# First batch of a state-space and expert layer: step size of batch two moved from POOL to VectorE, its silu in two places, four weight splits moved up

## The reference

```python
def attn(x):                                    # 8 heads of 64, state of 64
    z = x @ Wz                                  # 128 -> 256
    ssm_in = x @ Win                            # B (64), C (64), dt_raw (8), X (512)
    delta = softplus(dt_raw + dt_bias)          # the step size, per token and head
    y = ssd_scan(X, delta, B, C, A_log) + D_param * X
    z_gated = silu(z) @ Wzg                     # 256 -> 512
    return (y * z_gated) @ Wout                 # 512 -> 128
x1 = layernorm(x + attn(x))
# 12 experts, each 128 -> 512 -> 128; three routers take the top 3 and softmax them
h = gelu(sum_e dw1[:, e] * (x1 @ W1[e].T))
y = sum_e dw2[:, e] * (h @ W2[e].T) + dw3 @ b2
out = layernorm(x1 + y)
```

## Time and profile before

| what | value |
|---|---|
| median of 3 runs | 1566.34 us |
| lowest and highest | 1566.17, 1568.41 us |
| the profiled execution's own time | 1565.38 us |
| its span, first to last instruction | 1563.7 us |
| mean granted TensorE clock | 0.998 of full speed |
| busy: TensorE, VectorE, POOL, ScalarE | 1545.0, 1108.0, 663.7, 598.1 us |

### The profile page before, as it was taken

How to read it: one execution, slowest core, us unless ns; L and a number is a source line. 1 busy time by engine, 2 the same in 40 slices (tenths; PEclk the granted TensorE clock), 3 DMA queues, 4 the chain that set the end, 5 groups by cost and what they waited for, 6 DMA issues and landing times.

```text
span 1563.7 us, 25298 instructions
## 1 busy us (share of the span) xinstructions
PE 1545.0 (99%) x8634; PEld 1249.2 (80%) x8634; DVE 1108.0 (71%) x3108; ACT 598.1 (38%) x1362; POOL 663.7 (42%) x755
## 2 busy tenths in 40 slices
PE   8999999999999999999999999999999999999998
PEld 6778788888888878888788888878888788887876
DVE  7577676877768687676776768777686776867755
ACT  6652424425144351533425244242443515335130
POOL 7681623616145270643616336162451715436040
PEclk9999999999999999999999999999999999999999
DMA  5350312304023040321403123040230403214020
GB/s 176 102 158 22 116 41 66 98 29 132 19 76 88 29 135 14 103 69 46 118 17 118 44 66 98 29 128 22 71 93 29 136 14 99 73 40 125 15 74 7
DMA packets 81600, 114.79 MB, mean 73 GB/s; under 512 B 10160, under 2 KB 37312, under 8 KB 81472
## 3 DMA queue, kind: packets, MB, share of 16 engines
q1 hardware_dynamic: 81472, 113.18, 24.9%
HBM read 108.02 MB, written 5.13 MB: 72 GB/s over the span
## 4 chain that ended last, share of the span: by engine, by line
PE 92%; POOL 4%; issue 1%; DVE 1%; DMA 1%; ACT 0%; SPq 0%; POOLq 0%; DVEq 0%; ACTq 0%
PE exp_bank L246 22%; PE exp_bank L248 22%; PE exp_bank L247 22%; PE mix_bank L893 4%; PE mix_bank L919 3%; PE mix_bank L246 3%; PE mix_bank L247 3%; PE mix_bank L248 3%; PE mix_bank L901 3%; PE mix_bank L790 1%; PE turn_bank L1224 1%; POOL w_lo L445 1%; PE mix_bank L738 1%; POOL Wt L853 1%; PE mix_bank L1010 1%
## 5 line engine op out<-in xcount | busy, mean ns | idle before, releaser
L1167 POOL TENSOR_TENSOR sp_lo<-fbuf,sp_hi 128x512 fp32r<-128x512 f32 (+2 forms) x203 | 246.6, 1218 | 179.3 <-ACT sp_hi L1164 112.7
L246 PE MATMUL exp_bank<-w_hi,sp_hi 128*128 128x512 f32 x768 | 307.5, 400 | 0.8 <-POOL sp_lo L1217 0.8
L246 PE MATMUL exp_bank<-sp_hi,w_hi 128*128 128x512 f32 x764 | 304.9, 399 | 2.2 <-POOL sp_lo L1167 2.0
L248 PE MATMUL exp_bank<-w_hi,sp_lo 128*128 128x512 f32 x768 | 303.2, 395 | 0.0
L247 PE MATMUL exp_bank<-w_lo,sp_hi 128*128 128x512 f32 x768 | 303.1, 395 | 0.0
L248 PE MATMUL exp_bank<-sp_hi,w_lo 128*128 128x512 f32 x764 | 300.5, 393 | 0.0
L247 PE MATMUL exp_bank<-sp_lo,w_hi 128*128 128x512 f32 x764 | 298.8, 391 | 0.0
L1264 DVE SCALAR_TENSOR_TENSOR acc<-exp_bank,dw,acc 128x128 f32<-128x128 f32 x384 | 132.2, 344 | 152.9 <-PE exp_bank L248 152.2
L1164 ACT CAST sp_hi<-fbuf 128x512 fp32r<-128x512 f32 (+2 forms) x203 | 120.0, 591 | 277.2 <-DVE fbuf L1134 217.2
L853 POOL TENSOR_TENSOR Wt<-Wt,Gh 128x512 f32<-128x512 f32 x128 | 184.9, 1446 | 23.0 <-DVE Wt L845 22.9
L246 PEld LDWEIGHTS exp_bank<-sp_hi,w_hi 128*128 128x128 f32 x764 | 143.6, 188 | 43.2 <-issue 8.0
(11 more groups left out here) (267 smaller groups left out, 2281.4 us busy)
## 6 DMA issues: line engine op xcount, KB each, us to landing
row_b<-dw_rows SPq DMA_DIRECT2D x190, 256.0 KB, 3.4
seg_b<-dA_rows SPq DMA_DIRECT2D x124, 256.0 KB, 3.6
ctd<-cum_rows SPq DMA_DIRECT2D x128, 96.0 KB, 3.3
x_in<-in_x SPq DMA_DIRECT2D x16, 256.0 KB, 2.8
result<-acc SPq DMA_DIRECT2D x15, 256.0 KB, 2.3
fbuf<-in_W1T SPq DMA_DIRECT2D x12, 256.0 KB, 4.2
acc<-in_W2T SPq DMA_DIRECT2D x5, 256.0 KB, 4.0
x_in<-in_W2T SPq DMA_DIRECT2D x3, 256.0 KB, 4.4
```

The source lines that it names most:

```text
L246: nc.tensor.matmul(ps, s_hi, m_hi, start=start and j == 0, stop=False)
L248: last = nc.tensor.matmul(ps, s_lo, m_hi, start=False, stop=stop and j == n - 1)
L1167: sig("xw_lo", PO.tensor_tensor(lo[:, cols], wide[e % 2][:, cols], hi[:, cols].bitcast(F32), ALU.subtract))
```

## The change

Three things are moved in the start, and none is removed.

1. `mix_step` of batch two is done by VectorE in place of POOL, in two parts: part 0 after the gate of head pair 2, part 1 behind the gate of the last head pair. `mix_step` lets ScalarE do its exp and its logarithm in separate calls; the logarithm comes behind the casts of weights 9 to 11.
2. silu(z) of batch two: the first half on VectorE stays ahead of `mix_out`, the second comes behind `route_stats`. ScalarE's cast of the second half comes behind its part of `route_stats`.
3. On POOL the splits 8 to 11 and the memset of `load_b2` follow directly on the last product of the mixture, where the step was.

```diff
-            if eng is AC:
+            if eng is AC and 0 in parts:
                 if table:
                     AC.preload_act_table_set(LOG_EXP)
                 wait(AC, "dt_v", b, 4)
                 sig("dt_s", AC.activation(e, e, ACT.Exp))
+            if eng is AC and 1 in parts:
                 wait(AC, "dt_v", b, 5)
                 sig("dt_s", AC.activation(m, u, ACT.Ln))
...
-        def mix_z(eng, b):
+        def mix_z(eng, b, ks=range(NK)):
-            for k in range(NK):
+            for k in ks:
...
-        def mix_silu_split(eng, b, on=PO):
+        def mix_silu_split(eng, b, on=PO, ks=range(NK)):
-            for k in range(NK):
+            for k in ks:
...
-            mix_step(DVE, nxt)
+            mix_step(DVE, nxt, on=DVE, parts=(0,))
             mix_y(DVE, b, NQ - 1)
-            mix_z(DVE, nxt)
+            mix_step(DVE, nxt, on=DVE, parts=(1,))
+            mix_z(DVE, nxt, range(1))
             mix_out(DVE, b)
             route_stats(DVE, b)
+            mix_z(DVE, nxt, range(1, NK))
             first_weights_ready(DVE)
             route_scale(DVE, b)
...
-            mix_step(AC, nxt, table=False)
+            mix_step(AC, nxt, table=False, parts=(0,))
             split_w(AC, range(9, 12))
+            mix_step(AC, nxt, parts=(1,))
             mix_z(AC, nxt)
             AC.preload_act_table_set(LOG_EXP)
-            mix_silu_split(AC, nxt)
+            mix_silu_split(AC, nxt, ks=range(1))
             mix_X(AC, nxt, [0], on=AC)
             route_stats(AC, b, table=False)
+            mix_silu_split(AC, nxt, ks=range(1, NK))
             mix_X(AC, nxt, [1], on=AC)
             first_weights_ready(AC)
...
                 if 0 < q < NQ - 1:
                     split_w(PO, [5 + q])
-            mix_step(PO, nxt)
             split_w(PO, range(8, 12))
             load_b2(PO)
             wait(PO, "x1", b)
             mix_silu_split(PO, nxt)
```

## The result

The changed kernel takes 1569.33 us (median of 20 runs, 1567.36 to 1571.65), the kernel before 1565.88 in 20 runs beside it (1562.41 to 1568.41). The ratio is 1.0026, with a 95% interval of 1.0019 to 1.0032: slower by 0.26%, which is clear of the noise and more than the forecast's 0.95 us. The range ended at 1569.3, just under the result.

The account below looks back on a forecast made before the run. The start of the scaling (56.77), behind POOL's weight splits, was taken to set the end. VectorE's held step-size operations would make it about 0.95 us later: 1566.34 + 0.95 = 1567.3 us, range 1564.3 to 1569.3.

Parts of the forecast that it names:

- the forecast's 0.95 us: Start of the scaling before the transposes: about 57.75 instead of 56.77, taken to delay everything by about 0.95 us.
- The gate at 46.9: Last head pair's gate on VectorE: waits only for TensorE, starting at about 46.9 instead of 48.51.
- The output product behind the spacers without a pause: TensorE's output product at the end of batch one's mixture: starts at 48.4, 0.8 us earlier.
- three held operations: VectorE behind the gate: three small step-size operations each last until a POOL split ends, 1.1 to 1.25 us each.
- No wait for POOL's splits before the scaling: Before the scaling: POOL's splits are done at 51.2, so `first_weights_ready` costs nothing.
- The add long after the output product: Residual add on VectorE: starts at 54.8, 1.7 us later than before, though TensorE's output is ready at 52.2.
- No cost by the moved casts and loads: ScalarE's moved casts end near 59.9, ahead of the transposes' end at 60.35; SP's b2 loads costed at nothing.
- Rival 1: VectorE behind the gate hardly held: scaling 1.5 us earlier, 1564.8 us, or 1563.2 with the clock; chance 0.24.
- the memset is no such obstacle: POOL's memset beside VectorE: does not hold small operations, since one took 0.16 us at 56.97 during it.
- rival 2: TensorE's pause before the transposes grows to 2.85 us, prolonging the slow clock: 1568.9 or 1570.6 us; chance 0.14.
- from 12 to 15 us the engine was busy 0.01 us and kept 1.00: Argument against the longer slow stretch: TensorE stood idle early in the kernel and its clock stayed at full rate.
- The price that I gave one more stretch: X and gate products after the transposes: another 3.3 us at clock 0.50 costs up to half, 1.65 us.

## Why the prediction was off

**Right.** The gate at 46.9 (47.20, of which 0.27 is TensorE's product ahead of it ending at 46.28 + 0.87 instead of 46.01 + 0.87, before anything that the change edits). The output product behind the spacers without a pause (48.53). The first two small operations held ahead of the gate, one of them by split 8. Then three held operations, one for each split left on POOL, 1.1 to 1.2 us each for two of them. No wait for POOL's splits before the scaling. The add long after the output product. No cost by the moved casts and loads (9.70 us behind the transposes at full clock, as before). The sign of the whole: no gain, a loss at the scaling. Rival 1, with VectorE hardly held, is excluded by the held rows and by the run in which the splits wait.

**The term that was mis-sized: +0.95 us for the scaling.** It is 1.34 to 1.71 (58.18 and 58.48 in two profiles, against 56.84 and 56.77). The step was "the memset is no such obstacle". The row that I took it from is an operation with two SBUF inputs; the one that met the memset here is a tensor_scalar, and it took 0.47 more, which the run with the memset moved away gave back. The kinds of operation were in the row and I did not weigh them; I also held both kinds to be stopped only by a POOL operation that reads. The Trainium skill, SBUF — State Buffer, section "Who interferes with whom", makes a difference there: an operation with two SBUF inputs contends only with a GpSimd one that reads SBUF, while tensor_scalar, copy and cast can, when their operands meet its conditions, run in a mode that uses the shared port pair and contends with GpSimd whatever that does. Three rows agree with it (1.60 with the memset and 1.13 without it for the tensor_scalar; 1.15 for the two-input operation that meets the memset at its end). The 0.27 from upstream comes on top in the first profile. The rest are small: free operations started every 0.29 us and not every 0.27, and one more gap of 0.17 behind the step.

**The step that failed: the clock, put at nothing in the sum, and the 0.14 given to rival 2.** The forecast adds 0.95 us of waiting and no clock; measured, the second stretch at 0.50 adds 1.4 us or more behind the transposes. The mechanism of rival 2 was written down as it went: the step size late, the pause before the transposes from 1.18 to 2.85 us (3.66), products slow beyond 64.5. I gave it little, because "from 12 to 15 us the engine was busy 0.01 us and kept 1.00". That was one execution of a thing that varies from one to the next; the second profile of the same kernel has the opposite. Rival 2's sum with one more stretch, 1568.9, comes nearest to the result. All five profiles with a pause over 3 us (3.19, 3.38, 3.66, 3.69, 3.79) show two stretches or more at 0.50; the nine with a pause of 0 to 2.24 us show none there (seven) or one (two).

**How the loss is made up.** Two terms: waiting, 1.34 to 1.71 us at the scaling, and clock, 12.35 to 12.56 us from the transposes to the turned input where before they took 9.70 or 10.92, that is 1.4 to 2.9. Together 2.8 to 4.6; measured, 3.45 between the medians and 4.1 (1.0026 x 1565.88) by the ratio. The runs hold the two apart: with the waiting and the pause filled (28 spacers) the ratio is 1.0005, with the pause and nothing else (4 spacers) 1.0019, with both 1.0026. The medians thus show the pause as a cause. The waiting is shown by the timelines, and by the medians only against the kernel before with its own pause filled (1.0005 [0.9996, 1.0014] beside 0.9988 [0.9978, 0.9998]). Which of the two is the larger part stays open. The price that I gave one more stretch, 1.65 at most, was of the right size (1.4 from the first profile to this one).

**What was overlooked in reading the profile before.** The reciprocal's wait of 4.11 us drew the eye. The gate alone moved 1.6 us earlier leaves the scaling at 56.72: POOL's work before its last split, the step size among it, was the chain. The change takes the step size away from POOL, which does end the splits at 51.4 instead of 56.7; but each of them then stops one of VectorE's operations, and the three together take 3.91 us where 0.53 does with the splits away (0.17, 0.18 and 0.18).

The Trainium skill, GPSIMD Engine Reference, section "Key points", has VectorE about twice as fast at elementwise work. That agrees with the split's subtraction (128x512: 0.63 us on VectorE at 49.22 in the run with two splits there, 1.26 on POOL). At 128x32 the advantage is smaller: a free two-input operation takes 0.19 us on VectorE and 0.25 on POOL, and they start every 0.29 and every 0.40 us. Beside POOL's splits it is turned round, 1.14 to 1.17 us, and that decided here.

**Open.** In most profiles the clock is low somewhere before 20 us or from 61 us, and where it is varies for one and the same kernel (the kernel before, twice). Only the profiled execution tells where; of the others the time and the mean clock are known. Most executions of the changed kernel (17 of 20) have a lower mean clock than its two profiles, so where their further slow stretches lie, and whether the change brought these, is open. For this reason the share of the clock in the 3.45 us is given as a bracket. That the pause makes the clock fall rests on the runs with 4 and with 28 spacers; why a pause of 1.18 us did it in one profile and one of 1.88 in another did not is open too.

## What to carry to other kernels

Before small dependent operations are moved to VectorE, look at what POOL does at that time: each may cost the rest of one POOL instruction, and in these rows the kind of both operations (two SBUF inputs, tensor_scalar, memset) says whether it does. Ask which queue releases last, which need not be the one with the longest wait: the wait of 4.11 us was worth nothing, and two splits fewer on POOL moved the scaling from 56.8 to 55.9. And where TensorE is held busy by spacers, lengthen them with whatever is made late ahead of them, since here a longer pause cost again behind it.

## What was unexpected in the hardware

The clock falls in different places for the same program: 61.2 to 64.6 us in one execution, 14.7 to 18.2 in another, with much the same pauses ahead of both. One stretch at 0.50 in batch two's products costs 1.2 us (10.92 against 9.70 us), two cost 2.5 to 2.9 (12.23 to 12.56), the three of one profile 3.3 (13.01), and none followed in the three profiles in which the spacers end 0.29 us or less before the transposes.

Also unexpected is how one-to-one the hold is: a chain of VectorE operations of 0.18 us each advances by one for each POOL instruction of 1.26 us, since POOL's next begins before VectorE's next arrives (48.91 against 49.09, 50.17 against 50.33). In two runs the first operation behind the gate slipped in ahead of a split, and the next three were held instead.
